# First layer norm's row factors sent through DRAM, its centring folded into the user weight, and another item order at the start

## The chip, the cores and the metric

The kernel runs on one core of one Trainium2 chip. A core has five engines with an instruction stream of their own: TensorE (PE in the profile, with its weight loads as PEld), VectorE (DVE), ScalarE (ACT), GpSimd (POOL) and SyncE (SP), and 16 DMA engines that the streams of SP and ACT feed. The metric is the device time of one execution in microseconds (us), less is better. Matrix data goes from DRAM to SBUF, products are summed up in PSUM banks of 512 floats a partition.

## The reference

```python
def layernorm(x): m = mean(x); v = var(x); return (x - m) / sqrt(v + 1e-5)      # over 128 features

h = item_feat @ W_item.T + b_item                     # items, 10000 x 128
b = layernorm(x) @ W_user.T + b_user                  # users, 10000 x 128
x = x + relu(adj @ h + b)                             # adj 10000 x 10000, float32, 400 MB
x = x + ffn(layernorm(x))                             # an LSTM over 10000 steps, gates on its output,
                                                      # cumulative sums from both sides
```

Reading `adj` once is 400 MB, and `adj @ h` is most of the arithmetic. The LSTM comes behind it and isn't touched by the change.

## The kernel before

**Layout.** Everything is held transposed: features on the 128 partitions, users along the free axis. `adj @ h` is computed in 20 blocks of 500 users (`NB`, `BW`), each in PSUM bank `psG[:, j % 2]`. A block sums over 78 chunks of 128 items and a tail of 16 items. The chunks come in 20 pieces of 4 or 3 (`r` = 0 to 19), and a piece in two halves (`h`) of 2 chunks: 500 KB of `raw`, one DMA. There are room for 4 pieces of `raw` and for 4 halves of `a_hi` and `a_lo`.

**Three matmuls a chunk.** Float32 values are split in a high part (type fp32r, made by ACT with a copy, `split_hi`) and a low part (DVE subtracts, `split_lo`). TensorE then multiplies high by high, low by high and high by low (the three lines 826 to 828). So each half passes DMA, ACT, DVE, PE in this order, and semaphores (`raw_in`, `hi_ready`, `lo_ready`, `halves_done`) tie them together. Each engine's order of work is written out by hand: the loop over `r` in `body` of each engine, with side work put in behind piece `AT[...]` (every block) or `FIRST[...]` (block 0).

**Items.** During block 0 the items are projected as well. A quad is 4 chunks (512 items, 256 KB; 20 quads). SP loads them in parts (`PARTS`) into `u`; TensorE projects quad `q` into `psI[:, q % 2]` (`item_quad`), DVE adds the bias (`item_sum_part`), ACT makes the high part (`item_hi_part`), DVE the low part (`item_lo_part`). Piece `r` of block 0 needs quad `r`; `item_quad(r + 3)` stands at the head of piece `r` on TensorE, and quads 0 to 2 stand ahead of block 0.

**First layer norm** (of x, one block ahead of its use). TensorE transposes the block's 500 users in 4 pieces of 125 into rows (`to_rows`, `psT`); DVE takes `bn_stats` of the rows, and forms the variance in three steps (`stats`, `pair_up`, `eps`); POOL raises it to the power -1/2 (`inv_std`, a 125x4 tile `rstd`); DVE forms the shift (`row_scale`); ACT scales and shifts the rows (`normalise`, 4 instructions); TensorE transposes back (`to_columns`, 4 transposes into `psV`); ACT copies to `v` (`out_v`); and TensorE adds `wu` times `v` to the block's sum at piece `AT["bias"]` = 2.

**Second layer norm** (of x + relu(...), one block behind) goes the same way through `psT`, `psV`, and ACT's `out_u`. A block of x1 is stored to DRAM by SP at `AT["store"]`, and the next block of x loaded at `AT["load"]`.

**Small loads** stand in ACT's queue: the weights, `late_loads(r)` among ACT's pieces of block 0.

## Time and profile before

| | |
|---|---|
| median of 3 runs | 1453.94 us (1453.23 to 1456.08) |
| profiled execution, its own time | 1454.52 us |
| its span, first to last instruction | 1452.7 us |
| granted TensorE clock, mean | 0.992 |
| busy: PE, DVE, ACT, POOL | 98%, 84%, 75%, 15% of the span |
| DMA, mean over the span | 295 GB/s |
| stage with the adjacency | about 0 to 1144 us |
| LSTM and output | from there to the end |

The page cuts the span into 40 slices of 36.3 us. In the first 31 of them TensorE is at nine tenths or more save the first, and the DMA engines move 323 to 396 GB/s; from then on DMA is nearly idle. The adjacency stage is 79% of the span.

### The profile page before, as it was taken

How to read it: one execution, taken by the hardware profiler on the slowest of the kernel's cores; microseconds unless marked ns; L12 is line 12 of the kernel's file. 1: busy time of each engine (PE TensorE's matmuls, PEld its weight loads, DVE VectorE, ACT ScalarE, POOL GpSimd, SP SyncE). 2: the span in 40 equal slices, each digit the busy share in tenths (PEclk: the TensorE clock that was granted, in tenths of full speed). 3: DMA queues.
4: the chain of work that ended last, by engine and by line, in shares of the span. 5: the costliest groups of instructions: out<-in, count | busy, mean ns of one | idle time of the engine just before them, and what ended most of it. 6: DMA issues, size and time to landing. Idle time of an engine off the chain costs nothing.

```text
span 1452.7 us, 26480 instructions
## 1 busy us (share of the span) xinstructions
PE 1420.6 (98%) x7556; PEld 1222.4 (84%) x7556; DVE 1221.7 (84%) x2051; ACT 1092.8 (75%) x1602; POOL 214.7 (15%) x193
## 2 busy tenths in 40 slices
PE   7999999999999999999999999999999899999994
PEld 6878888888888888888888888888888799999994
DVE  7998888888889888888888888888989666676667
ACT  5678778878878878887887887887788576556662
POOL 0000010001001001001000000100100132027775
PEclk9999999999999999999999999999999999999997
DMA  9899999999999999999999999999999203000003
GB/s 373 330 323 357 395 363 356 390 366 351 392 361 359 387 366 363 376 372 371 370 363 384 364 361 393 358 359 393 359 356 389 100 0 141 0 2 0 1 0 142
DMA packets 129397, 428.00 MB, mean 295 GB/s; under 512 B 15763, under 2 KB 30420, under 8 KB 129238
## 3 DMA queue, kind: packets, MB, share of 16 engines
q1 hardware_dynamic: 127776, 426.43, 77.8%
q10 hardware_dynamic: 1590, 1.18, 0.2%
q8 instruction: 17, 0.28, 0.1%
q14 instruction: 14, 0.11, 0.0%
HBM read 417.30 MB, written 10.24 MB: 294 GB/s over the span
## 4 chain that ended last, share of the span: by engine, by line
PE 91%; DVE 4%; POOL 2%; issue 2%; DMA 1%; ACT 0%; POOLq 0%; SPq 0%; DVEq 0%
PE psG L826 24%; PE psG L827 24%; PE psG L828 24%; PE psZ L948 8%; PE psZ L934 2%; PE psZ L936 2%; PE psZ L938 2%; DVE a_lo L1107 1%; PE psG L844 1%; PE psT L792 1%; PE psV L800 1%; PE psI L872 1%; POOL own L516 1%; PE psZ L954 1%; POOL own L519 1%
## 5 line engine op out<-in xcount | busy, mean ns | idle before, releaser
L619 ACT ACTIVATE a_hi<-raw 128x1000 fp32r<-128x1000 f32 (+1 forms) x800 | 812.6, 1031 | 221.7 <-PE psG L828 215.3
L1107 DVE TENSOR_TENSOR a_lo<-raw,a_hi 128x1000 fp32r<-128x1000 f32 (+1 forms) x800 | 907.1, 1169 | 68.4 <-ACT a_hi L619 56.0
L826 PE MATMUL psG<-a_hi,item_hi 128*128 128x500 f32 x1560 | 620.1, 398 | 1.0 <-DVE a_lo L1107 0.8
L827 PE MATMUL psG<-a_lo,item_hi 128*128 128x500 f32 x1560 | 605.4, 388 | 0.0
L828 PE MATMUL psG<-a_hi,item_lo 128*128 128x500 f32 x1560 | 604.0, 387 | 0.0
L826 PEld LDWEIGHTS psG<-a_hi,item_hi 128*128 128x128 f32 x1560 | 293.1, 188 | 62.5 <-issue 5.4
L827 PEld LDWEIGHTS psG<-a_lo,item_hi 128*128 128x128 f32 x1560 | 293.4, 188 | 58.7 <-issue 4.4
L828 PEld LDWEIGHTS psG<-a_hi,item_lo 128*128 128x128 f32 x1560 | 292.8, 188 | 59.1
L445 POOL TENSOR_TENSOR rstd<-var,minus_half 125x4 f32<-125x4 f32 x40 | 76.1, 1903 | 1048.9 <-DVE var L1089 1048.9
L948 PE MATMUL psZ<-hist,wh 128*128 (+1 forms) x1264 | 168.0, 276 | 1.2 <-DVE hist L1275 1.1
L948 PEld LDWEIGHTS psZ<-hist,wh 128*128 128x128 f32 x1264 | 155.1, 192 | 1.8 <-issue 1.6
L704 ACT ACTIVATE psZ<-psZ 128x250 f32<-128x250 f32 x158 | 57.4, 363 | 62.2 <-PE psZ L948 60.0
L936 PE MATMUL psZ<-u_lo,wx_hi 128*128 (+1 forms) x312 | 97.4, 314 | 0.0
L934 PE MATMUL psZ<-u_hi,wx_hi 128*128 (+1 forms) x312 | 93.7, 302 | 0.0
L938 PE MATMUL psZ<-u_hi,wx_lo 128*128 (+1 forms) x312 | 87.3, 281 | 0.0
L1076 DVE BATCH_NORM_STATS2 moments<-psT 125x6 f32<-125x128 f32 x156 | 34.7, 285 | 48.5 <-PE psT L792 48.5
L1275 DVE SCALAR_TENSOR_TENSOR hist<-go,psZ 128x125 f32 (+1 forms) x160 | 45.4, 284 | 35.6 <-ACT psZ L713 34.7
L1260 DVE SCALAR_TENSOR_TENSOR psZ<-psZ,C 128x125 f32<-128x125 f32 x158 | 46.5, 295 | 33.4 <-ACT psZ L704 31.3
L708 ACT ACTIVATE go<-psZ 128x250 f32<-128x250 f32 x158 | 59.4, 376 | 7.0 <-PE psZ L948 0.4
L713 ACT ACTIVATE psZ<-C 128x125 f32<-128x125 f32 x158 | 43.6, 276 | 24.6 <-DVE C L1270 21.0
L936 PEld LDWEIGHTS psZ<-u_lo,wx_hi 128*128 128x128 f32 x312 | 59.1, 190 | 0.8
L938 PEld LDWEIGHTS psZ<-u_hi,wx_lo 128*128 128x128 f32 x312 | 58.8, 189 | 0.8
(171 smaller groups left out, 840.6 us busy)
## 6 DMA issues: line engine op xcount, KB each, us to landing
raw<-in_adj_main SPq DMA_DIRECT2D x760, 500.0 KB, 5.7
raw<-in_adj_main SPq DMA_DIRECT2D x40, 250.0 KB, 3.3
x_copy<-xb SPq DMA_DIRECT2D x20, 250.0 KB, 5.8
u<-x_copy SPq DMA_DIRECT2D x1, 5000.0 KB, 14.5
out<-u SPq DMA_DIRECT2D x25, 200.0 KB, 2.4
xb<-in_xT SPq DMA_DIRECT2D x18, 250.0 KB, 5.3
u<-in_itemT SPq DMA_DIRECT2D x8, 512.0 KB, 10.7
raw<-in_adj_tail SPq DMA_DIRECT2D x60, 31.2 KB, 2.9
```

The lines of the kernel that those rows point to most:

```text
L445: pool.tensor_tensor(rstd[:, :], var[:, :], minus_half[0:SW, :].to_broadcast([SW, SUB]), ALU.pow).then_inc(ln_rstd, 1)
L619: nc.scalar.activation(a_hi[:, s % CUT, 0:n], raw[:, r % RAW, at:at + n], ACT.Copy)\
L704: nc.scalar.activation(tb(g, 0, 2).rearrange("p (q k) -> p q k", k=KG), zb(g, 0, par), ACT.Tanh)\
L708: nc.scalar.activation(go[:, g, :].rearrange("p (q k) -> p q k", k=KG), zb(g, 1, par), ACT.Tanh)\
L826: pe.matmul(bank, w_hi, hi, start=(c == 0), stop=False)
L827: pe.matmul(bank, w_hi, lo, start=False, stop=False)
L828: last = pe.matmul(bank, w_lo, hi, start=False, stop=False)
L934: pe.matmul(z, w_hi, hi, start=(q % 2 == 0), stop=False, skip_group_check=True)
L936: pe.matmul(z, w_hi, lo, start=False, stop=False, skip_group_check=True)
L938: pe.matmul(z, w_lo, hi, start=False, stop=False, skip_group_check=True)
L948: last = pe.matmul(psZ[:, 2 * par + bank, at:at + KG], wh[:, q * HID:(q + 1) * HID], hist[:, row, g * KG:(g + 1) * KG], start=False, stop= ...
L1107: last = dve.tensor_tensor(a_lo[:, s % CUT, 0:m], raw[:, r % RAW, at:at + m], a_hi[:, s % CUT, 0:m].bitcast(f32), ALU.subtract)
```

## The change

It has three parts.

1. **The first layer norm leaves its transposes back.** The mean is taken out by the weight: TensorE multiplies `centre` (identity minus 1/128) with `wu` once, at piece 3 of block 0, and DVE copies the product over `wu`. What is left is one factor 1/sqrt(v + eps) for each user, and users lie along the free axis. POOL writes it into a tile of its own, `rstd1` (125x4). ACT's queue stores that tile to DRAM (`send_rstd`, 125 packets of 16 bytes) and, four pieces later (three in block 0), loads it back to all 128 partitions (`spread_rstd`, 128 packets of 2000 bytes) into `factors`, which is the tile `sq`. DVE multiplies x by it into `v` (`scale_user`), reading the factors with a step of 4 floats. DVE's `row_scale`, ACT's four `normalise` instructions, TensorE's `to_columns` and ACT's `out_v` of this norm are gone.
2. **Places.** `scaled` is at piece 3, `bias` goes from piece 2 to 5, `rows1` to `eps1` one piece earlier, `load` from 11 to 10, `wx` from 10 to 12. In block 0 the bias goes from 7 to 11.
3. **The items at the start.** Parts of two quads from the first on, and they are loaded at every second piece from piece 3 on, where they were loaded behind each of the first nine pieces. Only quads 0 and 1 are projected ahead of block 0; quad 2 stands between the halves of piece 0 and quad 3 behind them. On ACT the first `split_hi` stands ahead of the first item part, and on DVE the first `split_lo` ahead of the low part of quad 0 and the sum of quad 1.

```diff
-PARTS = (0, 1, 3, 5, 7, 9, 11, 13, 15, 17, QUADS)
+PARTS = (0, 2, 4, 6, 8, 10, 12, 14, 16, 18, QUADS)
+PART_AFTER = {0: (1,), 1: (2,), **{2 * i - 3: (i,) for i in range(3, len(PARTS) - 1)}}
-AT = dict(relu=1, x1=2, bias=2, rows2=3, stats2=4, pair2=5, eps2=5, scale2=6, norm2=7, back2=8, out2=10,
-          rows1=12, stats1=13, pair1=14, eps1=14, scale1=15, norm1=16, back1=17, out1=19,
-          store=7, load=11, wx=10)
+AT = dict(relu=1, x1=2, scaled=3, bias=5, rows2=3, stats2=4, pair2=5, eps2=5, scale2=6, norm2=7, back2=8, out2=10,
+          rows1=11, stats1=12, pair1=13, eps1=13, send=15, spread=19, store=7, load=10, wx=12)
-FIRST = dict(rows=0, stats=1, scale=2, norm=3, back=4, out=5, bias=7)
+FIRST = dict(rows=0, stats=1, send=3, centre=3, centred=4, spread=6, scaled=9, bias=11)
...
+            def send_rstd(m):
+                act.wait_ge(ln_rstd, m + 1)
+                act.dma_start(rstd_dram[0:1, :].rearrange("o (p s) -> p (o s)", s=SUB), rstd1[:, :]).then_inc(rstd_stored, 16)
+            def spread_rstd(j):
+                act.wait_ge(rstd_stored, 16 * (j + 1))
+                act.dma_start(factors[:, :], rstd_dram[0:1, :].to_broadcast([P, BW])).then_inc(rstd_spread, 16)
...
+            def scale_user(j):
+                dve.wait_ge(rstd_spread, 16 * (j + 1))
+                by_row = factors[:, :].rearrange("p (r s) -> p s r", s=SUB)
+                xs, vs = (t.rearrange("p (s r) -> p s r", s=SUB) for t in (xb[:, j % 2, :], v[:, :]))
+                dve.tensor_tensor(vs, xs, by_row, ALU.mult).then_inc(v_ready, 1)
...
-                        if r + AHEAD < QUADS:
+                        if 0 < r < QUADS - AHEAD:
                             item_quad(r + AHEAD)
...
+                        if items and r == 0:
+                            item_quad(2 + h)
-                    if items and r == FIRST["back"]:
-                        to_columns(0)
+                    if items and r == FIRST["centre"]:
+                        pe.wait_ge(wu_in, 32)
+                        pe.matmul(psW[:, 0:HID], centre[:, :], wu[:, :], start=True, stop=True).then_inc(wu_psum, 1)
-                    if has1 and r == AT["back1"]:
-                        to_columns(2 * j + 1, u_ready if has2 else v_ready, j if has2 else 1)
...
+                    if items and r == FIRST["centred"]:
+                        dve.wait_ge(wu_psum, 1)
+                        dve.tensor_copy(wu[:, :], psW[:, 0:HID]).then_inc(wu_ready, 1)
```

How the order changes. VectorE's stream at the start of block 0, before (psI holds a projected quad, L1121 is its sum, L1107 the low part of a half of the adjacency, L1140 the low part of a quad):

```order
1 L1216 COPY bi<-psW 128x128
2 L1121 TENSOR_TENSOR u<-psI,bi 128x512 x2
3 L1140 TENSOR_TENSOR item_lo<-u,item_hi 128x512
4 L1107 TENSOR_TENSOR a_lo<-raw,a_hi 128x1000
5 L1121 TENSOR_TENSOR u<-psI,bi 128x512
6 L1107 TENSOR_TENSOR a_lo<-raw,a_hi 128x1000
7 L1140 TENSOR_TENSOR item_lo<-u,item_hi 128x512
8 L1107 TENSOR_TENSOR a_lo<-raw,a_hi 128x1000
```

and in the changed kernel (the same three are L1144, L1130, L1163):

```order
1 L1247 COPY bi<-psW 128x128
2 L1144 TENSOR_TENSOR u<-psI,bi 128x512
3 L1130 TENSOR_TENSOR a_lo<-raw,a_hi 128x1000
4 L1163 TENSOR_TENSOR item_lo<-u,item_hi 128x512
5 L1144 TENSOR_TENSOR u<-psI,bi 128x512
6 L1130 TENSOR_TENSOR a_lo<-raw,a_hi 128x1000
7 L1144 TENSOR_TENSOR u<-psI,bi 128x512
8 L1163 TENSOR_TENSOR item_lo<-u,item_hi 128x512
```

The first low part of the adjacency now stands behind one sum, where it stood behind two sums and the low part of quad 0.

TensorE's stream in the steady loop, before, at the end of piece 17 of a block (L826 to L828 are the three matmuls of a chunk, L800 the four transposes back of the first norm):

```order
520 L826 MATMUL psG<-a_hi,item_hi 128x500
521 L827 MATMUL psG<-a_lo,item_hi 128x500
522 L828 MATMUL psG<-a_hi,item_lo 128x500
523 L796 REGISTER_ALU
524 L800 MATMUL psV<-ident,normed 128x125 x4
525 L815 REGISTER_ALU
526 L826 MATMUL psG<-a_hi,item_hi 128x500
```

and at the same place in the changed kernel (L842 to L844):

```order
520 L842 MATMUL psG<-a_hi,item_hi 128x500
521 L843 MATMUL psG<-a_lo,item_hi 128x500
522 L844 MATMUL psG<-a_hi,item_lo 128x500
523 L831 REGISTER_ALU
524 L842 MATMUL psG<-a_hi,item_hi 128x500
```

The transposes and their wait are gone, and the next piece follows at once. The transposes back of the second norm, at piece 8, are still there.

VectorE's stream in the steady loop from the x1 sum (L1099) to the statistics of the second norm, before:

```order
115 L1099 TENSOR_TENSOR xb<-xb,un_bb 128x500
116 L1104 REGISTER_ALU
117 L1107 TENSOR_TENSOR a_lo<-raw,a_hi 128x1000
118 L1104 REGISTER_ALU
119 L1107 TENSOR_TENSOR a_lo<-raw,a_hi 128x1000
120 L1104 REGISTER_ALU
121 L1107 TENSOR_TENSOR a_lo<-raw,a_hi 128x1000
122 L1104 REGISTER_ALU
123 L1107 TENSOR_TENSOR a_lo<-raw,a_hi 128x1000
124 L1074 ISA
125 L1076 BN_STATS moments<-psT 125x6 x4
```

and in the changed kernel (L1122 is the x1 sum, L1130 the low part):

```order
116 L1122 TENSOR_TENSOR xb<-xb,un_bb 128x500
117 L1127 REGISTER_ALU
118 L1130 TENSOR_TENSOR a_lo<-raw,a_hi 128x1000
119 L1127 REGISTER_ALU
120 L1130 TENSOR_TENSOR a_lo<-raw,a_hi 128x1000
121 L1115 ISA
122 L1118 ISA
123 L1118 TENSOR_TENSOR v<-xb,sq 128x500
124 L1127 REGISTER_ALU
125 L1130 TENSOR_TENSOR a_lo<-raw,a_hi 128x1000
126 L1127 REGISTER_ALU
127 L1130 TENSOR_TENSOR a_lo<-raw,a_hi 128x1000
```

The multiplication at 123 is new, with its wait for the spread factors ahead of it; two halves' low parts and then the statistics are queued behind it.

## Rows read from the trace of the kernel before

**Rows 1.** The page: busy us, share and instructions of each engine.

```profile
PE 1420.6 (98%) x7556; PEld 1222.4 (84%) x7556; DVE 1221.7 (84%) x2051; ACT 1092.8 (75%) x1602; POOL 214.7 (15%) x193
```

**Rows 2.** Waits over the whole span: total us, times, longest.

```profile
ACT a_hi L619 <- PE psG L828: 215.3, 559, 2.8
...
ACT a_hi L619 <- DMA raw<-in_adj_main: 3.0, 5, 1.3
```

**Rows 3.** Windows: us, busy PE, PEld, DVE, ACT, POOL, clock, DMA, GB/s.

```profile
20.00:40.00 20.00, 19.82 (x109) 16.85 (x108) 19.90 (x33) 14.49 (x20) 2.04 (x2) 1.00 1.03 407
...
300.00:400.00 100.00, 100.00 (x456) 82.91 (x455) 88.48 (x111) 81.17 (x96) 5.79 (x3) 1.00 0.98 373
```

**Rows 4.** Timeline of TensorE in a steady block: start us, duration us.

```profile
570.53 0.60 PE L792 MATMUL psT<-ident,xb 128*125 128x128 f32 x4
...
604.74 0.39 PE L826 MATMUL psG<-a_hi,item_hi 128*128 128x500 f32 x1
...
614.66 0.39 PE L828 MATMUL psG<-a_hi,item_lo 128*128 128x500 f32 x1
614.89 0.59 PE L800 MATMUL psV<-ident,normed 125*128 125x125 f32 x4
...
615.55 0.39 PE L827 MATMUL psG<-a_lo,item_hi 128*128 128x500 f32 x1
...
626.14 0.60 PE L792 MATMUL psT<-ident,xb 128*125 128x128 f32 x4
```

**Rows 5.** Groups by line: busy us, mean ns, idle before.

```profile
L605 ACT ACTIVATE u<-psV 128x480 f32 (+1 forms) x19 | 20.1, 1060 | 0.0
...
L1099 DVE TENSOR_TENSOR xb<-xb,un_bb 128x500 f32 (+1 forms) x19 | 12.8, 672 | 0.0
...
L597 ACT ACTIVATE v<-psV 128x500 f32<-128x500 f32 x20 | 11.4, 571 | 2.4 <-PE psV L800 2.4
```

**Rows 6.** Timeline of TensorE from the start on, the lines that mark progress.

```profile
4.66 2.08 PE L872 MATMUL psI<-wi,u 128*128 128x128 f32 x8
9.62 3.52 PE L872 MATMUL psI<-wi,u 128*128 128x128 f32 x16 [2.89 <-DMA u<-in_itemT]
13.81 1.16 PE L872 MATMUL psI<-wi,u 128*128 128x128 f32 x8 [0.66 <-DMA u<-in_itemT]
14.72 0.47 PE L826 MATMUL psG<-a_hi,item_hi 128*128 128x500 f32 x1
...
26.65 0.48 PE L826 MATMUL psG<-a_hi,item_hi 128*128 128x500 f32 x1
```

**Rows 7.** Timeline of ScalarE, then of VectorE, in the same stretch.

```profile
8.11 1.95 ACT L619 ACTIVATE a_hi<-raw 128x1000 fp32r<-128x1000 f32 x2
...
11.74 0.69 DVE L1121 TENSOR_TENSOR u<-psI,bi 128x512 f32<-128x512 f32 x1 [4.20 <-PE psI L872]
...
12.95 1.19 DVE L1107 TENSOR_TENSOR a_lo<-raw,a_hi 128x1000 fp32r<-128x1000 f32 x1
```

**Rows 8.** DMA of the first 40 us: GB/s in slices of 1 us; issues with us to landing.

```profile
GB/s 0 33 247 349 358 402 405 409 392 260 319 410 412 428 416 414 416 415 412 410 400 409 402 406 401 411 413 413 421 413 413 394 404 412 400 413 413 391 391 418
...
raw<-in_adj_main SPq DMA_DIRECT2D x23, 500.0 KB, 10.2
u<-in_itemT SPq DMA_DIRECT2D x8, 512.0 KB, 10.7
```

**Rows 9.** DMA issues of the whole span: KB each, median us to landing.

```profile
x_copy<-xb SPq DMA_DIRECT2D x20, 250.0 KB, 5.8
```

**Rows 10.** DMA from 40 to 45 us, where 128 packets of 4 bytes run.

```profile
q10 hardware_dynamic: 144, 0.00, 1.7%
...
fwc<-in_fw ACTq DMA_DIRECT2D x1, 0.5 KB, 5.6
```

**Rows 11.** Timeline of VectorE in a steady block, around the second norm's statistics.

```profile
598.64 1.20 DVE L1107 TENSOR_TENSOR a_lo<-raw,a_hi 128x1000 fp32r<-128x1000 f32 x1
601.56 0.89 DVE L1076 BATCH_NORM_STATS2 moments<-psT 125x6 f32<-125x128 f32 x4 [1.71 <-PE psT L792]
```

More of the change, by code:

```diff
@@ L95, in program @@
     ds = bass.ds
+    rstd_dram = nc.dram_tensor("rstd_copy", (1, BW), f32).ap()
     x1_dram = nc.dram_tensor("x1_copy", (P, N), f32).ap()
@@ L163, in program @@
         rstd = sb("rstd", [SW, SUB], f32, first)
+        rstd1 = sb("rstd1", [SW, SUB], f32, first)
+        factors = sq
         shift_rows = sb("shift_rows", [SW, SUB], f32, first)
@@ L401, in load_block @@
                         sp.dma_start(xb[:, (j + 1) % 2, :], xT[:, ds((j + 1) * BW, BW)]).then_inc(xb_in, 16)
-            load_block(0, wait=False, move=False, items={r: (r + 1,) for r in range(len(PARTS) - 2)})
+            load_block(0, wait=False, move=False, items=PART_AFTER)
             with nc.sync.Fori(1, NB - 1) as j:
@@ L586, in relu, with normalise @@
                     .then_inc(relu_done, 1)
-            def normalise(m):
-                act.wait_ge(ln_scale, m + 1)
+            def normalise(count):
+                act.wait_ge(ln_scale, count)
                 for s in range(SUB):
@@ L631, in body @@
                         late_loads(r)
[L632 to L635 removed]
+                    if items and r == FIRST["send"]:
+                        send_rstd(0)
+                    if items and r == FIRST["spread"]:
+                        spread_rstd(0)
                     if has2 and r == AT["norm2"]:
[L637 removed]
+                        normalise(j)
                     if has2 and r == AT["out2"]:
[L639 to L643 removed]
+                        out_u(j, odd, pair)
+                    if has1 and r == AT["send"]:
+                        send_rstd(2 * j + 1)
+                    if has1 and r == AT["spread"]:
+                        if items:
+                            act.wait_ge(item_ready, QUADS)
+                        spread_rstd(j + 1)
             def item_hi_part(q):
@@ L787, in _, with to_rows @@
         def _(pe):
-            def to_rows(m, par):
-                if not (isinstance(m, int) and m == 0):
-                    pe.wait_ge(ln_normed, m)
+            def to_rows(par, reader=None, count=0):
+                if reader is not None:
+                    pe.wait_ge(reader, count)
                 for s in range(SUB):
@@ L1193, in body @@
                         eps(0)
-                    if items and r == FIRST["scale"]:
-                        row_scale(0)
+                    if items and r == FIRST["centred"]:
+                        dve.wait_ge(wu_psum, 1)
+                        dve.tensor_copy(wu[:, :], psW[:, 0:HID]).then_inc(wu_ready, 1)
+                    if items and r == FIRST["scaled"]:
+                        scale_user(0)
+                    if has2 and r == AT["scaled"]:
+                        scale_user(j)
                     if has2 and r == AT["x1"]:
@@ L1211, in body @@
                         eps(2 * j + 1)
-                    if has1 and r == AT["scale1"]:
-                        row_scale(2 * j + 1)
             dve.wait_ge(bi_psum, 1)
```

72 lines of the change are left out of this document (34 added, 38 removed).

## The prediction

> **What bounds the kernel now.** I read the page's busy shares first. TensorE is busy in 98% of the span, VectorE in 84%, ScalarE in 75% [rows 1]. A busy share alone doesn't prove a bound, so the list of waits comes next: ScalarE waited 215.3 us for TensorE to give back a slot of `a_hi`, and 3.0 us in all for the adjacency's DMAs [rows 2]. So the chain DMA, ACT, DVE, PE is held up from its end: TensorE is the bound, and the others wait for its slots. The windows say by how much. From 300 to 400 us PE is busy in all 100 us, DVE in 88.5, ACT in 81.2, and DMA moves 373 GB/s; from 20 to 40 us, with the items on top, DMA moves 407 GB/s and DVE is busy in 19.9 of 20 us [rows 3]. So there are two regimes: the steady blocks, bound by PE with 12% left on DVE and about 8% on DMA, and block 0's beginning, where DVE and DMA are full as well.
>
> The timeline of TensorE gives its pace: 44 starts from 604.74 to 614.66, 0.2255 us a matmul [rows 4]. From one block's transposes to rows at piece 12 (570.53) to the next's (626.14) are 55.61 us [rows 4]. In them lie 234 matmuls and the tail's one (52.99 us), two sets of transposes to rows, two sets back, and the bias. What leaves TensorE's stream there shortens the block.
>
> **The transposes back: 20 sets.** One set of 4 stands between the starts at 614.66 and 615.55 [rows 4]. Without it those two starts would be 2 x 0.2255 = 0.45 us apart, and they are 0.89 apart: a set costs 0.44 us. (The set's own 0.59 us [rows 4] is the other end, but its last part overlaps the next matmul.) There are 20 sets of the first norm, one a block: 20 x 0.44 = 8.8 us. The transposes to rows stay and cost the same one piece earlier. The bias matmul costs the same at piece 5 as at piece 2; it is what is left of the block, 55.61 - 52.99 - 4 x 0.44 = 0.86 us. The new block is 55.17.
>
> **What leaves ScalarE** is 4 `normalise` instructions and `out_v` (0.57 us, [rows 5]) a block, and what comes is two issues of DMAs in its queue. ACT waits for TensorE anyway, so I count nothing. Its new waits: at piece 15 for POOL's power, whose input DVE finishes at piece 13; at piece 19 for the store to land, 4 pieces after its issue. Behind them stand the next `split_hi`, and behind those DVE and PE; they hurt only if a landing takes more than the distance.
>
> **The round trip through DRAM.** Four pieces are 48 matmuls, 10.8 us, from store to load; from the load's issue to DVE's use at piece 3 of the next block there are four again. A DMA of 250 KB to DRAM took 5.8 us [rows 9]; a load of 128 packets of 4 bytes 5.6 us [rows 10]. Both hops fit with 5 us left. In block 0 the hops are 3 pieces of 12 matmuls and a quad, about 3.6 us each, again 10.8 us, but there the queues are full: loads of the adjacency took 10.2 us there and those of the items 10.7 [rows 8]. Those wait behind their own queue's backlog; ACT's small loads don't, as the 5.6 us at 41 us show. I take 6 to 7 us for each hop, so nothing is late.
>
> What the two transfers cost the DMA engines: the spread is 0.256 MB, 0.6 us at 407 GB/s [rows 3]. For packets of 16 bytes the nearest row is that of 144 packets (128 of 4 bytes and the completions) that took 1.7% of 16 engines in 5 us, 1.36 engine-us, 9 ns each [rows 10]: 125 are 1.2 engine-us. That was reading from DRAM, this writes to it, which no row shows at that size. With 20.6 MB a block (40 halves, the stored and the loaded block), DMA needs 50.6 us at 407 GB/s and has 55.2. So the additions may reach 4.6 us a block before DMA becomes the bound. I take them as hidden.
>
> The Trainium skill, page "DMA: Bandwidth & Descriptors" (sections "Specifications" and "Why a DMA increments its semaphore by 16 and not by 1"), says that below 512 bytes a write turns into a read and a write, and that a DMA runs on the largest number of engines up to 16 that divides its slowest dimension: for 125 partitions 5 engines with 25 packets each. By the 9 ns of rows 10 that would be 0.2 us on each of five engines, and the sum stays; no row here shows either. It makes the first rival below easier to come true, which I left at 0.03.
>
> **What comes to VectorE.** `scale_user` multiplies 128x500. The like instruction with plain steps is 0.672 us [rows 5]. Its factors are read with a step of 16 bytes. For steps of that kind no read on DVE is in the rows; on ACT, writing with a large step took 1.060 us for 480 elements against 0.571 for 500 plain ones [rows 5], 1.9 times. So the price is between 0.67 and 1.28 us; I take 0.7, nearest to the row of the same engine. It replaces `row_scale`. At piece 3 DVE has room: before the statistics at 601.56 it stood idle for 1.71 us, waiting for TensorE's transposes [rows 11]. Those come up to 0.86 us sooner now, since the bias stands behind them; 1.71 - 0.86 = 0.85 us of room is left, and `v` isn't needed before piece 5. Even 1.28 us overdraws it by 0.4, less than the 0.65 us that 12% of idle time are worth in two pieces. Hidden; zero in the steady blocks.
>
> The Trainium skill, page "SBUF — State Buffer" (the note on SBUF cachelines), says that SBUF has lines of 16 bytes and that each access that goes to a new line pays a penalty. Here every factor would be on a new line. By that rule the upper price holds, and by the plain row the lower; the sum is the same by both, block 0 apart, which is a rival below.
>
> **TensorE in block 0 gets one matmul more,** `centre` by `wu`, a 128x128 of the items' kind: a quad of 4 such took 0.91 us of stream (13.81 to 14.72 [rows 6]), so 0.25 us. DVE's copy of the result, 0.3 us, falls at piece 4.
>
> **The start.** Before, PE waits for quads 1 and 2 to land and projects them from 9.62 (after 2.89 us idle), DVE can add their bias at 11.74 after 4.20 us idle, and the first low part of the adjacency starts at 12.95, although ACT had made the first two high parts from 8.11 on [rows 6, 7]. The first adjacency matmul is at 14.72, the first of piece 3 at 26.65 [rows 6]. I run the new order through with the durations of these rows, in us:
> - Quads 0 and 1 come with one 512 KB DMA. From the rates in rows 8 the summed bytes are 0.63 MB at 4, 1.4 at 6, 2.2 at 8, 3.6 MB at 12, then 0.41 a us, and loads landed 1.5 us behind their place. So: items 5.4, first halves 7.1 and 8.7, quads 2 and 3 10.2, piece 1 12.0 and 13.3, quads 4 and 5 14.8.
> - PE projects quads 0 and 1 from 5.4 to 9.3, at the slow early pace of rows 6 (2.08 us for one). DVE: sum of 0 to 8.1, low part of half 0 (1.1) 8.3 to 9.4, low part of quad 0 to 10.0, sum of quad 1 to 10.6, half 1 to 11.8.
> - PE: half 0 from 10.1, quad 2, half 1 from 12.3, quad 3, rows, then quad 4 (landed 14.8), piece 1 from about 15.7. DVE goes on without a gap: quads, four `bn_stats`, the variance; half 4 is ready at 19.9, half 6 at 23.3. PE starts piece 3 at 23.8.
>
> So piece 3 starts 26.65 - 23.8 = 2.85 us earlier. From there on PE isn't starved: half 6 of the adjacency would land at 18.9, halves 8 and 10 at 23.4 and 25.8, each 2 to 3 us before DVE gets to it, since the items now take 0.26 MB a piece and not 0.5. Bounds: if the matmuls of the first half run at half pace, 1.4 us less; if DVE were the only limit from 8.3 on (12.95 - 8.3), up to 4.6. I take 2.85.
>
> **The sum:** 8.8 + 2.85 - 0.25 = 11.4 us. Profiled time 1454.52 - 11.4 = 1443.1; the median of the runs is 0.6 below the profiled one, so 1442.5. I add 0.3 for DVE's copy and multiplication in block 0, where DVE is full: **1442.8 us**. The LSTM behind it is the same, and I expect the same time of it.
>
> **Rivals.**
> 1. *DMA becomes the bound* (slower). For: the DMA share is 0.98 already; a load from one spot of DRAM by 128 packets and small writes are in no row. Against: 407 GB/s in block 0. It decides from 4.6 us of additions a block, with 0.6 for the spread, 4.0 are left for 125 packets of 16 bytes, 8 on each of 16 engines: 0.5 us a packet. At 1 us each a block needs 50.6 + 0.6 + 8 = 59.2, 3.6 more than the 55.61 of before; 19 x 3.6 = 68, less 2.6 at the start: 1519. By the skill's rule of five engines, above, it would decide from 4.0 / 25 = 160 ns a packet, an estimate.
> 2. *The round trip is late* (slower). It decides from landings of 10.8 us. The 10.2 to 10.7 us of rows 8 are close. If the spread takes 12 us in each block, DVE stalls 1.2 us, and its lead takes perhaps 0.4: (0.8 - 0.44) x 19 = +6.8, less 2.3 at the start: 1458. Late in block 0 alone: 1444.
> 3. *VectorE pays for the step, and block 0 gives less.* 0.6 us more for the multiplication at piece 9 of block 0, 1.4 for matmuls at half pace at the start, 0.5 that DVE doesn't catch up: 1445.3.
> 4. *The start gives nothing*, since DMA, full from 5 us on [rows 8], holds back block 0 whatever the order. Against it: ACT waited 3.0 us for loads [rows 2], with twice the items ahead of the adjacency. 1442.8 + 2.6 = 1445.4.
> 5. *The steady blocks give nothing*, since DVE's and DMA's loops, at 88% and 92% [rows 3], take over at once: 1453.9 - 2.6 = 1451.3.
>
> **How the numbers follow.** Forecast 0.60, rival 1 0.03, rival 2 0.06 (half of it slower, half in block 0 only), rival 3 0.13, rival 4 0.12, rival 5 0.06. Under 0.2% (2.9 us) I call it no change, about what can be told. Faster: 0.60 + 0.13 + 0.12 + half of rival 2, 0.03 = 0.88; same: 0.06; slower: 0.03 + 0.03 = 0.06. The forecast's own range is 1440.8 (the start's upper bound) to 1444.2; with rivals 3 and 4 to 1446, and part of 5: 1440.5 to 1448.
>
> **What would show it.** In the changed profile: 19 groups of transposes into `psV`, not 39; matmuls still 0.2255 us apart; the first adjacency matmul near 10 us and piece 3 near 24; the steady block shorter by 0.44 us; `v<-xb` at 0.7 (or 1.3) us, and little waiting for it on the spread; landings of the two new DMAs under 8 us. I am wrong if ACT waits for `raw` by tens of us in the steady blocks (rival 1), if DVE waits ahead of `v` (rival 2), or if PE waits for `a_lo` at every block's piece 3 or 4 (rivals 3, 5).

## The result, and the profile after

The changed kernel takes 1445.34 us (median of 4 runs, 1444.94 to 1446.79) against 1453.79 us (4 runs), a ratio of 0.994 with a 95% interval of 0.9928 to 0.9952. The forecast was 1442.8 us, its range 1440.5 to 1448.0. So it is faster, as forecast, by 8.45 us where 11.4 less 0.3 were expected. The profiled execution took 1444.94 us, its span is 1443.1.

The page's busy shares of the changed kernel answer to [rows 1]. TensorE has 78 instructions less: 80 transposes are gone, and the product of `centre` and `wu` shows as 2. VectorE has 21 us more:

```profile
PE 1412.8 (98%) x7478; PEld 1214.0 (84%) x7478; DVE 1242.8 (86%) x2052; ACT 1067.8 (74%) x1502; POOL 214.5 (15%) x193
```

The waits of the changed kernel (engine, what waited, for whom: us in all, times, longest) answer to [rows 2]. ScalarE still waits mostly for TensorE, but its waits for the adjacency's DMAs went from 3.0 us to 33.9, in 89 places:

```profile
ACT a_hi L634 <- PE psG L844: 208.4, 585, 2.8
...
ACT a_hi L634 <- DMA raw<-in_adj_main: 33.9, 89, 1.9
...
PEld psG L842 <- DVE a_lo L1130: 4.4, 11, 0.6
```

TensorE's timeline at the start (start, duration, engine, line, operation, tiles, count) answers to [rows 6]. The first matmul of the adjacency is at 10.03 where 10.1 was forecast, that of piece 3 at 24.09 where 23.8 was (26.65 before), and the centring takes 0.22 us (26.89 to 27.11):

```profile
5.39 3.78 PE L890 MATMUL psI<-wi,u 128*128 128x128 f32 x16
10.03 0.50 PE L842 MATMUL psG<-a_hi,item_hi 128*128 128x500 f32 x1 [0.86 <-DVE item_lo L1163]
...
15.90 0.48 PE L842 MATMUL psG<-a_hi,item_hi 128*128 128x500 f32 x1
...
24.09 0.47 PE L842 MATMUL psG<-a_hi,item_hi 128*128 128x500 f32 x1
...
26.89 0.38 PE L853 MATMUL psW<-wu,centre 128*128 128x128 f32 x2
27.11 1.06 PE L890 MATMUL psI<-wi,u 128*128 128x128 f32 x8
```

The multiplication by the factors, as the groups of instructions give it (busy us in all, mean ns of one, idle time before it): 1.075 us and no wait for the spread. The like instruction with plain steps takes 0.672 [rows 5]. The 19 groups of transposes into `psV` are there as 76:

```profile
L1118 DVE TENSOR_TENSOR v<-xb,sq 128x500 f32<-128x500 f32 x20 | 21.5, 1075 | 0.0
...
L816 PE MATMUL psV<-ident,normed 125*128 125x125 f32 x76 | 11.2, 270 | 0.0
```

The best ruler is the tail's matmul, the last of each block. In the changed kernel blocks 0 to 3 end here:

```profile
84.34 0.38 PE L835 MATMUL psG<-a_hi,item_hi 80*128 80x500 f32 x1
...
141.36 0.39 PE L835 MATMUL psG<-a_hi,item_hi 80*128 80x500 f32 x1
...
196.58 0.40 PE L835 MATMUL psG<-a_hi,item_hi 80*128 80x500 f32 x1
...
251.88 0.39 PE L835 MATMUL psG<-a_hi,item_hi 80*128 80x500 f32 x1
```

Beside the same line of before, in us:

| | before | after | gained | forecast |
|---|---|---|---|---|
| end of block 0 | 88.39 | 84.34 | 4.05 | 3.18 |
| block 1 | 55.79 | 57.02 | -1.23 | 0.44 |
| a steady block, undisturbed | 55.60 | 55.22 | 0.38 | 0.44 |
| blocks 2 to 18, sum | 945.26 | 939.51 | 5.75 | 7.48 |
| block 19 | 54.73 | 54.77 | -0.04 | 0 |
| end of the stage | 1144.17 | 1135.64 | 8.53 | 11.1 |

(3.18 is 2.85 + 2 x 0.44 - 0.25 - 0.3.) The LSTM behind it took 1.07 us less in this execution (307.46 us for 308.53). The change has no part in that: over the 14 profiled executions of this document what follows the stage takes either 307.3 to 307.5 us (six of them, the changed kernel's here among them) or 308.3 to 308.5 (eight, that of before among them). So of the 9.6 us between the two profiled executions 8.53 belong to the change.

So three things are to be explained: block 1 loses 1.8 us against a steady block; a set of transposes is worth 0.38 and not 0.44; and among the steady blocks there are stalls (one block takes 55.73 us), 0.77 us in all. In block 1 it is ScalarE that is late, for `raw`. Its timeline in the changed kernel, where before it had no wait for a DMA at all between 78 and 100 us:

```profile
85.77 0.66 ACT L595 ACTIVATE un_bb<-psG,bu 128x500 f32<-128x500 f32 x1
88.23 1.04 ACT L634 ACTIVATE a_hi<-raw 128x1000 fp32r<-128x1000 f32 x1 [1.80 <-DMA raw<-in_adj_main]
89.88 1.04 ACT L634 ACTIVATE a_hi<-raw 128x1000 fp32r<-128x1000 f32 x1 [0.61 <-DMA raw<-in_adj_main]
91.13 1.04 ACT L634 ACTIVATE a_hi<-raw 128x1000 fp32r<-128x1000 f32 x1 [0.21 <-DMA raw<-in_adj_main]
```

The spread was issued at 80.88 and landed 8.0 us later, in the midst of that. TensorE still had finished halves to work on; its first wait in block 1 comes 4 us after ScalarE fell idle at 86.4, for VectorE's low part:

```profile
90.56 0.50 PE L842 MATMUL psG<-a_hi,item_hi 128*128 128x500 f32 x1 [0.23 <-DVE a_lo L1130]
```

### The profile page after: what moved, and what is told of

Same layout as the page of the kernel before. It is cut to its first block, busy times and chain, and to the rows that moved or that the text cites. A ratio compares the mean times of both kernels' runs of the same rounds, so it can differ in the third digit from the quotient of the medians.

```text
span 1443.1 us, 26187 instructions
## 1 busy us (share of the span) xinstructions
PE 1412.8 (98%) x7478; PEld 1214.0 (84%) x7478; DVE 1242.8 (86%) x2052; ACT 1067.8 (74%) x1502; POOL 214.5 (15%) x193
## 4 chain that ended last, share of the span: by engine, by line
PE 91%; DVE 3%; issue 2%; POOL 2%; DMA 1%; ACT 0%; POOLq 0%; DVEq 0%; SPq 0%; ACTq 0%
PE psG L842 24%; PE psG L843 24%; PE psG L844 24%; PE psZ L965 8%; PE psZ L951 2%; PE psZ L953 2%; PE psZ L955 2%; PE psG L863 1%; PE psT L810 1%; PE psI L890 1%; DVE a_lo L1130 1%; POOL own L526 1%; PE psZ L971 1%; DMA raw<-in_adj_main 1%; POOL own L529 1%
## 5 line engine op out<-in xcount | busy, mean ns | idle before, releaser
L634 ACT ACTIVATE a_hi<-raw 128x1000 fp32r<-128x1000 f32 (+1 forms) x800 | 821.8, 1031 | 244.8 <-PE psG L844 208.4
L1130 DVE TENSOR_TENSOR a_lo<-raw,a_hi 128x1000 fp32r<-128x1000 f32 (+1 forms) x800 | 911.0, 1170 | 74.5 <-ACT a_hi L634 55.2
L842 PE MATMUL psG<-a_hi,item_hi 128*128 128x500 f32 x1560 | 620.5, 398 | 2.1 <-DVE a_lo L1130 1.1
L844 PE MATMUL psG<-a_hi,item_lo 128*128 128x500 f32 x1560 | 604.7, 388 | 0.0
L842 PEld LDWEIGHTS psG<-a_hi,item_hi 128*128 128x128 f32 x1560 | 293.5, 188 | 66.9 <-issue 5.6
L844 PEld LDWEIGHTS psG<-a_hi,item_lo 128*128 128x128 f32 x1560 | 293.2, 188 | 59.4
L951 PEld LDWEIGHTS psZ<-u_hi,wx_hi 128*128 128x128 f32 x312 | 59.0, 190 | 0.0
## 6 DMA issues: line engine op xcount, KB each, us to landing
u<-in_itemT SPq DMA_DIRECT2D x9, 512.0 KB, 10.1
```

Of the source, the lines that this page charges most:

```text
L634: nc.scalar.activation(a_hi[:, s % CUT, 0:n], raw[:, r % RAW, at:at + n], ACT.Copy)\
L842: pe.matmul(bank, w_hi, hi, start=(c == 0), stop=False)
L844: last = pe.matmul(bank, w_lo, hi, start=False, stop=False)
L951: pe.matmul(z, w_hi, hi, start=(q % 2 == 0), stop=False, skip_group_check=True)
L1130: last = dve.tensor_tensor(a_lo[:, s % CUT, 0:m], raw[:, r % RAW, at:at + m], a_hi[:, s % CUT, 0:m].bitcast(f32), ALU.subtract)
```

## The experiments

Theory A: TensorE's stream bounds the blocks, and what is lost is lost to the two new transfers, where VectorE and the ring of `raw` have no lead. Theory B: VectorE (1.08 us for the multiplication, and the new order) loses it. The times of before beside them are 1453.67 us (experiments 1 to 3), 1454.53 (4 to 7), 1454.78 (8 to 10) and 1454.45 (11 and 12). A table of all profiles stands behind the experiments.

**1. The new start alone**: the kernel before with part 3 of the change and nothing of parts 1 and 2.

```diff
-PARTS = (0, 1, 3, 5, 7, 9, 11, 13, 15, 17, QUADS)
+PARTS = (0, 2, 4, 6, 8, 10, 12, 14, 16, 18, QUADS)
+PART_AFTER = {0: (1,), 1: (2,), **{2 * i - 3: (i,) for i in range(3, len(PARTS) - 1)}}
...
-            item_quad(2)
...
```

> The kernel before with the new order of block 0 alone (parts of the items, two quads ahead of the adjacency, DVE's and ACT's order); the first norm keeps its transposes back. Theory A (PE, with a debt): the start gains 2.5 us at piece 3 and keeps nearly all of it; block 1 loses at most 0.5, because the loss of 1.7 us there comes with the spread. 1451.3 to 1451.8. Rival B (block 0 and 1 together have a bound of their own, DVE or DMA, which the earlier start only reaches sooner): block 1 gives back 1.5 us or more, and 1452.5 to 1453.3 is left.

Measured: 1451.9 us, ratio 0.999 (0.9981 to 0.9999). In its profile block 0 ends 2.52 us earlier, block 1 takes 55.78 us as before, and all is kept to the end of the stage (1141.65). Theory A's reading holds. The profiled execution is the fastest of the 11, though, and the median lies 0.1 us above the expected range: by the medians the start alone is worth 1.8 us.

```profile
85.87 0.39 PE L821 MATMUL psG<-a_hi,item_hi 80*128 80x500 f32 x1
...
141.65 0.39 PE L821 MATMUL psG<-a_hi,item_hi 80*128 80x500 f32 x1
```

**2. The factors alone**: the changed kernel with the start of before (the diff above the other way round).

> The changed kernel with the old order of block 0: only the row factors through DRAM. Theory A: steady blocks of 55.22 us, 0.39 less than before each, 18 x 0.39 = 7.0, block 0 shorter by 0.4 to 0.8, block 1 longer by 1 to 1.7 since the spread sits in its beginning: 1446.6 to 1447.4. Rival B: block 1 takes 55.2 to 55.5 and the kernel is 1445.8 to 1446.3, that is, start and factors together lose what each keeps alone.

Measured: 1448.87 us, ratio 0.9967 (0.9957 to 0.9978). Block 0 ends at 88.23, block 1 takes 55.38, the steady ones 55.22 with four stalls of 0.2 us and one of 0.5; the stage ends at 1138.48, 5.69 us earlier. That is neither expectation: block 1 hardly loses, as in B, but stalls of 1.4 us lie elsewhere, and ScalarE waits 32.3 us for `raw`. Neither part alone makes block 1 long. Block 0 gains only 0.16 us here; its first adjacency matmul starts at 15.74, 1.02 us later than before, and the first four start 0.41 to 0.57 us apart.

**3. The spread's bytes taken away.**

```diff
-                act.dma_start(factors[:, :], rstd_dram[0:1, :].to_broadcast([P, BW])).then_inc(rstd_spread, 16)
+                if isinstance(j, int) and j == 0:
+                    act.dma_start(factors[:, :], rstd_dram[0:1, :].to_broadcast([P, BW])).then_inc(rstd_spread, 16)
+                else:
+                    act.dma_start(factors[0:1, :], rstd_dram[0:1, :]).then_inc(rstd_spread, 16)
```

> The changed kernel, but from block 1 on the spread loads only one partition's row of factors (2 KB for 256 KB); the other partitions multiply by old values, so the first norm of blocks 1 to 19 is left wrong. Nothing else moves. If the spread's bytes delay the adjacency (theory A), block 1 falls from 57.0 to 55.5 us or less, ACT's 33.9 us of waits for raw fall below 15, and the time is 1443.0 to 1443.8. If they are hidden (rival: the prefetch ran dry by itself), block 1 stays within 0.3 of 57.0 and the time within 0.5 of 1445.3.

Measured: 1443.7 us, ratio 0.9933 (0.992 to 0.9947). Block 0 ends at 84.31 as in the changed kernel, block 1 takes 55.38, and every block from 2 to 18 takes 55.21 to 55.23. The stage ends 2.44 us earlier than in the changed kernel. ScalarE's waits in it:

```profile
ACT a_hi L637 <- PE psG L847: 226.8, 640, 2.8
...
ACT a_hi L637 <- DMA raw<-in_adj_main: 13.2, 24, 1.6
```

VectorE still pays its 1.08 us here, so theory B falls: with no spread beside the adjacency that price costs the steady blocks nothing and block 1 at most 0.16 us (before the change, too, block 1 was 0.19 us longer than a steady block). The windows from 84 to 88 us, and of their first half (busy time of each engine and count, granted clock, DMA share, GB/s), show what the spread does to its neighbours. First the changed kernel, then this one:

```profile
84.00:88.00 4.00, 4.00 (x19) 3.10 (x18) 3.91 (x4) 2.43 (x3) 0.00 (x0) 1.00 0.78 254
84.00:86.00 2.00, 2.00 (x10) 1.44 (x9) 2.00 (x3) 2.00 (x3) 0.00 (x0) 1.00 0.63 186
```

```profile
84.00:88.00 4.00, 4.00 (x19) 3.10 (x18) 4.00 (x5) 3.54 (x5) 0.00 (x0) 1.00 0.98 363
84.00:86.00 2.00, 2.00 (x10) 1.45 (x9) 2.00 (x3) 2.00 (x3) 0.00 (x0) 1.00 0.99 351
```

In these 4 us DMA moved 0.44 MB less with the spread in flight, although the 254 GB/s hold bytes of the spread too. In the first two of them the compute engines do the same work in both kernels, and 0.33 MB are missing already, so the gap isn't only the echo of a late ScalarE. The DMA share falls with the rate, 0.63 for 0.99: the DMA engines stood idle in part of that time. Why they did, no run shows. The forecast had counted the spread's bytes alone.

**4. 500 packets of 4 bytes and plain steps.**

```diff
-                act.dma_start(rstd_dram[0:1, :].rearrange("o (p s) -> p (o s)", s=SUB), rstd1[:, :]).then_inc(rstd_stored, 16)
+                with nc.allow_non_contiguous_dma(reason="500 packets of 4 bytes"):
+                    act.dma_start(rstd_dram[0:1, :].rearrange("o (s p) -> p (o s)", s=SUB), rstd1[:, :]).then_inc(rstd_stored, 16)
...
-                by_row = factors[:, :].rearrange("p (r s) -> p s r", s=SUB)
-                xs, vs = (t.rearrange("p (s r) -> p s r", s=SUB) for t in (xb[:, j % 2, :], v[:, :]))
-                dve.tensor_tensor(vs, xs, by_row, ALU.mult).then_inc(v_ready, 1)
+                dve.tensor_tensor(v[:, :], xb[:, j % 2, :], factors[:, :], ALU.mult).then_inc(v_ready, 1)
```

> The changed kernel with the factors stored transposed: 500 packets of 4 bytes in the place of 125 of 16, and scale_user reads them with plain steps. DVE's multiplication falls from 1.08 to 0.67 us. Theory (the spread's bytes are what block 1 pays, DVE has room): block 1 stays over 56.5 us, steady blocks 55.22, time within 0.5 of 1445.3; more small packets may make it longer, by 0.5 to 2 us over all. Rival (DVE's price of 1.08 us in block 1 is part of it): block 1 is 0.4 or more shorter, 1444.5.

Measured: 1550.31 us, ratio 1.0626 (1.0565 to 1.0687). Both expectations were wrong by 100 us. Blocks take 58.8 to 64.3 us, though VectorE's multiplication fell to 0.671. The store of 2 KB, issued at 622.34, nearly stops the adjacency; in these windows of that kernel the last two columns are the DMA share and GB/s:

```profile
624.00:626.00 2.00, 2.00 (x10) 1.66 (x9) 2.00 (x3) 1.36 (x3) 0.00 (x0) 1.00 1.36 292
626.00:628.00 2.00, 2.00 (x10) 1.69 (x9) 1.94 (x2) 1.69 (x2) 0.00 (x0) 1.00 1.03 43
628.00:630.00 2.00, 2.00 (x10) 1.67 (x9) 1.71 (x3) 1.42 (x2) 0.00 (x0) 1.00 1.23 36
630.00:632.00 2.00, 2.00 (x10) 1.65 (x10) 0.94 (x1) 0.00 (x0) 0.00 (x0) 1.00 0.50 32
632.00:634.00 2.00, 2.00 (x11) 1.46 (x9) 0.68 (x1) 0.62 (x1) 0.00 (x0) 1.00 0.51 103
634.00:636.00 2.00, 0.87 (x4) 0.41 (x3) 0.00 (x0) 0.00 (x0) 0.00 (x0) 1.00 0.91 281
```

Against 407 GB/s these windows lack 3.3 MB, 8 us of DMA for one store, by this estimate 16 ns of all 16 engines for each packet, where the forecast took 9 ns of one. (Against the steady 373 GB/s of [rows 3] it is 2.9 MB.) In block 0 ScalarE even waited 7.8 us for the store to land: with 500 packets the round trip is late once, as in the second rival. This is the first rival's mechanism; it is real, but the changed kernel's packets lie on its cheap side. In the changed kernel the store is issued at 624.31, and there is only a dip:

```profile
624.00:626.00 2.00, 2.00 (x11) 1.67 (x10) 2.00 (x3) 1.70 (x2) 0.28 (x1) 1.00 1.01 346
626.00:628.00 2.00, 2.00 (x11) 1.65 (x10) 2.00 (x3) 1.36 (x3) 0.00 (x0) 1.00 1.10 282
628.00:630.00 2.00, 2.00 (x10) 1.68 (x9) 1.93 (x2) 1.69 (x2) 0.00 (x0) 1.00 0.78 199
```

The profile's pages also count the packets of ScalarE's queue, for before, the changed kernel and this one in turn (packets, MB, share):

```profile
q10 hardware_dynamic: 1590, 1.18, 0.2%
...
q10 hardware_dynamic: 7070, 6.34, 1.6%
...
q10 hardware_dynamic: 14570, 6.34, 1.5%
```

A block has 274 packets more than before in the changed kernel, and 649 in this one. With 144 for the spread (128 and 16 completions, as the prediction reads [rows 10]), 125 + 5 and 500 + 5 are left for the store. Five completions for 16 speak for a store that runs on 5 of the 16 engines, as the prediction considered.

The Trainium skill, page "DMA: Bandwidth & Descriptors" (section "Specifications"), says that a write of less than 512 bytes is turned into a read and a write. The run agrees that small writes are dear; that it was this that stopped the other packets, no run here shows.

**5. One packet stored in the place of 125.**

```diff
+                if isinstance(m, int) and m == 0:
...
+                else:
+                    act.dma_start(rstd_dram[0:1, 0:SUB], rstd1[0:1, :]).then_inc(rstd_stored, 16)
```

> The changed kernel, but from block 0's piece 15 on the store writes only one partition's 4 factors (one packet of 16 bytes for 125); the first norm of blocks 1 to 19 is left wrong. Theory: the store is cheap, block 1 and the time stay within 0.5 us of 57.0 and 1445.3, and the spread still lands in 7 to 8 us. Rival (125 small writes cost the DMA engines as much as the spread): block 1 falls by 0.5 us or more, ACT's waits for raw from 33.9 us to under 20, 1444.2.

Measured: 1445.81 us, ratio 0.9939 (0.9922 to 0.9956). The time says the store is cheap, the profile says more: ScalarE's waits for `raw` fall to 10.0 us, and of blocks 2 to 18 all but one (55.62) take 55.21 to 55.24. Block 0 ended at 86.54, though, and block 1 took 55.40. The 2.2 us arise at the start, and they look like TensorE's clock. In this execution the adjacency's first matmuls start 0.42 us apart, 500 columns at 1.2 GHz, and in the changed kernel's profile 0.23 us, the level of 2.4 GHz. All of TensorE's work is slow there, the weight loads too (0.33 us for 0.19) and the quad behind the matmuls (1.91 us for 1.05), so it isn't a matter of operands that land late. But the granted clock reads 1.00 in both. TensorE had stood idle for 0.86 us ahead of them in both. The timeline of this kernel, and below it a weight load of the changed kernel:

```profile
10.02 0.79 PE L845 MATMUL psG<-a_hi,item_hi 128*128 128x500 f32 x1 [0.86 <-DVE item_lo L1166]
...
11.02 0.62 PE L847 MATMUL psG<-a_hi,item_lo 128*128 128x500 f32 x1
11.03 0.33 PEld L845 LDWEIGHTS psG<-a_hi,item_hi 128*128 128x128 f32 x1
11.44 0.62 PE L845 MATMUL psG<-a_hi,item_hi 128*128 128x500 f32 x1
11.86 0.62 PE L846 MATMUL psG<-a_lo,item_hi 128*128 128x500 f32 x1
```

```profile
10.60 0.19 PEld L842 LDWEIGHTS psG<-a_hi,item_hi 128*128 128x128 f32 x1
```

That costs block 0 2.2 us. Block 1 loses nothing here, so blocks 0 and 1 together end at 141.94, and at 141.36 in the changed kernel.

**6. The spread twice** (the second into `normed`, which is overwritten before it is read).

```diff
+                act.wait_ge(extra_in, 16 * count)
...
+                if not (isinstance(j, int) and j == 0):
+                    act.dma_start(normed[:, 0:BW], rstd_dram[0:1, :].to_broadcast([P, BW])).then_inc(extra_in, 16)
```

> The changed kernel with every spread from block 1's on issued twice (the second into a buffer that is overwritten before it is read): 256 KB more a block. If DMA is close behind PE (theory: the removed spread gave back 2.4 us), each steady block loses 0.3 to 1.5 us, block 1 1.5 us more, ACT's waits for raw rise over 100 us: 1452 to 1475. If the 4.6 us of room that the prediction counted are there, only block 1 pays (58.5) and the time is 1446.5 to 1447.5.

Measured: 1456.33 us, ratio 1.0006 (0.9996 to 1.0016). Steady blocks take 55.2 to 56.5 us, and ScalarE waits 55.3 us for `raw`; the wait for the second copy, which the edit adds ahead of `normalise`, shows in no row. One more quarter of a megabyte a block, 1.2% of its bytes, eats the whole gain. So the 4.6 us of room that the forecast counted aren't there for a spread.

**7. A set of transposes twice**, the second norm's.

```diff
-                for s in range(SUB):
+                for s in (*range(SUB), *range(SUB)):
                     last = pe.transpose(psV[:, s * SW:(s + 1) * SW], normed[0:SW, s * HID:(s + 1) * HID],
```

> The changed kernel with the second norm's 4 transposes back issued twice in blocks 1 to 19. It gives a set's price on TensorE by itself. By the starts in the trace of before (0.89 - 0.45) a set is 0.44 us, by the blocks' difference 0.39: a steady block of 55.66 or of 55.61 us, 19 times, and 1453.7 or 1452.7.

Measured: 1454.34 us, ratio 0.9999 (0.999 to 1.0009). The undisturbed blocks take 55.63 to 55.65 us, 0.42 more for a set. In the profile, whose execution is the slowest of the ten, stalls of 4.6 us come on top, up to 57.2 us a block. Perhaps a stretched block meets the transfers at other places; that is not shown.

**8. The changed kernel once more**, beside the next two.

> The changed kernel itself once more, for the spread between executions: block 0's last matmul was at 84.3 us in it and in one variant, and at 86.2 to 86.5 in two others whose block 0 is the same. Expected 1445.3 within 0.8; block 0 and 1 together end between 141.0 and 142.2 us whichever way block 0 falls, ACT's waits for raw are 25 to 40 us.

Measured: 1447.34 us (5 runs, 1446.98 to 1450.22), ratio 0.996 (0.9946 to 0.9973), 2 us above the first four. Blocks 0 and 1 end at 84.33 and 140.74, ScalarE waits 34.6 us for `raw`, and one steady block takes 57.16. The stage ends 1.41 us later than in the first profile: block 1 takes 0.61 less and the stalls 2.03 more. The other 1.0 us between the two profiled executions is the LSTM's longer time. So the changed kernel's time scatters by 2 us and more: through stalls that fall differently in each execution, and through the LSTM's two lengths.

**9. 16 packets of 128 bytes.** VectorE turns the 125x4 factors in a 128x32 tile into 4 rows of 32 for each of four groups of partitions; four DMAs store them, and the spread then has them in the order in which VectorE reads x. Two more things change with it: the multiplication has plain steps, and in the steady blocks the store stands one piece later (16 for 15).

```diff
+                by_quarter = rstd_dram[0, :].rearrange("(s b r) -> b s r", s=SUB, b=4)
+                for b in range(4):
+                    act.dma_start(by_quarter[b], turned[32 * b:32 * b + SUB, :]).then_inc(rstd_stored, 16)
...
+                dve.transpose(turned[:, :], rstd32[:, :]).then_inc(rstd_turned, 1)
...
-                by_row = factors[:, :].rearrange("p (r s) -> p s r", s=SUB)
+                by_row = factors[:, :].rearrange("p (s r) -> p s r", s=SUB)[:, :, 0:SW]
```

> The changed kernel with the factors turned by VectorE (one 32x32-block transpose of a 128x32 tile, before the store) and stored by 4 DMAs of 4 packets of 128 bytes in the place of one of 125 packets of 16 bytes; the spread has 2 KB rows as before, and scale_user reads with plain steps. Theory (each small packet written costs the DMA engines much more than its bytes; 4 bytes 500 times cost 8 us of them): ACT's waits for raw fall from 33.9 to 10 us, steady blocks all 55.22, multiplication 0.67 us, 1443.7 to 1444.6. Rival (VectorE's transpose and four issues on ScalarE's queue cost as much as they save; the store was never the trouble, the spread is): ACT's waits stay over 25 us, 1445 to 1446.5.

Measured: 1443.81 us (5 runs, 1443.42 to 1445.67), ratio 0.9933 (0.9919 to 0.9946), 3.5 us under the changed kernel in experiment 8, and its slowest run is under the other's fastest. Against the changed kernel's first measurement (1445.34, ratio 0.994) it is 1.5 us, or 1.0 by the ratios, and there the intervals overlap. Blocks 2 to 18 take 55.21 to 55.24 us without one stall, block 1 still 56.35. That the packets did it, and not the cheaper multiplication, rests on experiment 5, where the multiplication cost 1.07 us and the stalls were gone all the same. The groups of its two VectorE operations and its waits:

```profile
L1132 DVE TENSOR_TENSOR v<-xb,sq 128x500 f32<-128x500 f32 x20 | 13.5, 674 | 0.0
...
L1126 DVE STREAM_TRANSPOSE turned<-rstd 128x32 f32<-128x32 f32 x20 | 4.0, 202 | 0.0
```

```profile
ACT a_hi L642 <- PE psG L852: 226.3, 633, 2.8
...
ACT a_hi L642 <- DMA raw<-in_adj_main: 15.0, 33, 1.7
```

**10. The store twice** (the second to another place in DRAM).

```diff
+                act.dma_start(rstd_dram2[0:1, :].rearrange("o (p s) -> p (o s)", s=SUB), rstd1[:, :]).then_inc(rstd_stored, 16)
...
-                act.wait_ge(rstd_stored, 16 * (j + 1))
+                act.wait_ge(rstd_stored, 32 * (j + 1))
```

> The changed kernel with the store of the factors issued twice, the second time to another place in DRAM: 250 packets of 16 bytes a block for 125. If a small packet costs what packets4 showed (16 ns of the whole DMA each), a block has 2 us more of DMA, 54.8 of 55.2 us: ACT's waits for raw rise from 33.9 to over 80 us, steady blocks lose 0.2 to 1.5 us, 1449 to 1470. If only packets of 4 bytes are so dear, or the neighbours in one line of DRAM, nothing moves: 1445.3 within 1.

Measured: 1448.35 us (1444.89 to 1452.04), ratio 0.9951 (0.9936 to 0.9967), 1.0 over the changed kernel in experiment 8, less than the two kernels' runs scatter. ScalarE's waits stay at 30.9 us; the profiled execution, the slowest of the four, has stalls of 5 us in its steady blocks. The waits of over 80 us that follow from experiment 4's price of 16 ns of the whole DMA a packet didn't come, so that price doesn't carry over to packets of 16 bytes. What they cost is bounded, not settled: taking them away ends the stalls (experiments 5 and 9), doubling them adds a microsecond or nothing.

**11 and 12. TensorE kept busy at the start**, in the changed kernel and in that of experiment 9.

```diff
+            def keep_on(n):
+                for _ in range(n):
+                    pe.matmul(spare[:, 0:P], centre[:, :], ident[:, :], start=True, stop=True)
...
+            keep_on(10)
             pe.wait_ge(bi_in, 16)
...
             item_quad(1)
+            keep_on(8)
```

> The changed kernel with matmuls that nobody reads on TensorE: 10 of 128x128 ahead of the first bias row (TensorE idles there until 4.7 us) and 8 behind the second quad of items (it idles 0.86 us there). In three of the eight traces with the new start the adjacency's first 6 matmuls ran at half pace (0.42 us apart for 0.2255), and block 0 ended at 86.2 us for 84.3. Theory: it is TensorE's clock, which the fill keeps up: quads 0 and 1 take 2.1 us for 3.78, the first adjacency matmul is at 9.0 to 9.6, block 0 ends at 83.3 to 84.3 in every run, but block 1 gives part of it back, for DVE has no lead there: 1444.0 to 1445.3. Rival: the pace has another cause (operands still landing), the first matmuls stay as they are; 1445.5 to 1447.

> The kernel with 16 packets of 128 bytes (rows16) and the same fill on TensorE. If both parts add up, 1442.3 to 1443.4, with steady blocks of 55.22 us and ACT's waits for raw under 20 us. If the earlier start is all given back in block 1, 1443.8 as rows16.

Measured: 1448.21 us, ratio 0.9952 (0.9939 to 0.9965), and 1444.52 us, ratio 0.9932 (0.9919 to 0.9944): no gain in either. The pace did what the theory said, but I had the fill's length wrong: a float32 matmul counts twice in the profile, so 10 were 20 and took until 6.80 us, where 4.7 was to be reached. The timeline of experiment 11:

```profile
2.23 4.64 PE L879 MATMUL unused_bank<-ident,centre 128*128 128x128 f32 x20 [2.23 <-POOL centre L446]
6.80 0.53 PE L901 MATMUL psW<-bi_row,ones 1*128 1x128 f32 x2
7.25 2.05 PE L894 MATMUL psI<-wi,u 128*128 128x128 f32 x16
9.14 1.95 PE L879 MATMUL unused_bank<-ident,centre 128*128 128x128 f32 x16
10.98 0.50 PE L842 MATMUL psG<-a_hi,item_hi 128*128 128x500 f32 x1
11.32 0.39 PE L843 MATMUL psG<-a_lo,item_hi 128*128 128x500 f32 x1
```

The two quads take 2.05 us and not 3.78, and the adjacency starts at full pace, but 0.95 us late. Block 0 ends at 85.29 and 85.37, block 1 takes 55.39 in both. A fill half as long wasn't tried.

**The profiles side by side**, in us: end of block 0, length of block 1, what blocks 2 to 18 take above 55.22 each, pace of the adjacency's first matmuls, ScalarE's waits for `raw`. (In experiment 7 55.64 is taken for 55.22, in experiment 1 and before 55.60, the steady block there. In experiment 4 the tail's loads, 16.3 us, are counted with the waits.)

| | block 0 | block 1 | stalls | first matmuls | waits |
|---|---|---|---|---|---|
| before | 88.39 | 55.79 | 0.1 | full | 3.0 |
| 1, new start alone | 85.87 | 55.78 | 0.1 | full | 2.8 |
| 4, 500 packets | 90.46 | 60.71 | 102.6 | full | 125.5 |
| changed kernel | 84.34 | 57.02 | 0.8 | full | 33.9 |
| 8, again | 84.33 | 56.41 | 2.8 | full | 34.6 |
| 3, spread of one row | 84.31 | 55.38 | 0.0 | full | 13.2 |
| 9, packets of 128 bytes | 84.58 | 56.35 | 0.1 | full | 15.0 |
| 6, spread twice | 84.56 | 57.43 | 9.4 | full | 55.3 |
| 11, fill | 85.29 | 55.39 | 3.7 | full | 26.5 |
| 12, fill, 128 bytes | 85.37 | 55.39 | 0.0 | full | 8.9 |
| 5, one packet | 86.54 | 55.40 | 0.4 | half | 10.0 |
| 10, store twice | 86.13 | 56.91 | 5.1 | half | 30.9 |
| 7, set twice | 86.20 | 56.78 | 4.6 | half | 37.4 |
| 2, old start | 88.23 | 55.38 | 1.4 | half | 32.3 |

## Why the prediction was right, and where its terms were off

**TensorE as the bound: right.** Undisturbed steady blocks got shorter when work left TensorE's stream, and as long again when experiment 7 put a set in. **The size of a set was off:** 0.38 us by the blocks of before and after, 0.42 by experiment 7, for 0.44 by two starts [rows 4]. Over blocks 2 to 18 that is 7.48 - 5.75 - 0.77 (stalls) = 0.96 us of the missing 2.6. Why an added set costs more than a removed one is open; the other side work changed its place with the removal.

**The start: right.** Its 2.85 us came as 2.56 at piece 3, and 2.52 were kept when it was alone (experiment 1). The steps came as worked out: the second half's matmuls at 12.31 for 12.3, piece 1 at 15.90 for 15.7. The first quad at 5.39 for 5.4 holds some luck: TensorE waited for the bias row there, until 4.70, and not for the items. Block 0 as a whole gained 4.05 for 3.18. The 0.87 us more are open: the start alone gave 2.52 and the factors alone 0.16, with a late first matmul (experiment 2). Why both together give 4.05, no run shows. The bound of half pace, 1.4 us less, was not idle: it came true in experiments 5, 7 and 10, where block 0 ends 1.8 to 2.2 us later; of the changed kernel's own two profiles neither shows it.

**"I take them as hidden": this step failed.** The forecast weighed the two transfers by bytes and by the average of a block: 50.6 + 0.6 us of DMA for 55.2. (A block's 20.0 MB of adjacency with its two blocks of 0.256 MB are 20.5 MB, not 20.6; that changes nothing.) Three things were wrong with it.
- The spread costs its neighbours more than its bytes (experiment 3: 0.44 MB in 4 us), and a second one cost 9 to 11 us over the whole kernel (experiment 6, against 1447.34 and 1445.34), or 7 to 10 by the ratios.
- The average isn't what counts. VectorE is full until the end of block 0 (3.89 of 4 us from 80 to 84) and has little lead over TensorE, so loads of `raw` that come late in block 1 stop TensorE 4 us later (90.56). Block 1 came out 1.67 us worse than forecast. Without the spread (experiment 3) or without the new start (1 and 2) block 1 takes 55.4 to 55.8. That an end of block 0 a microsecond later is enough was only argued: experiments 5, 11 and 12 say so, 7 and 10 speak against it. Which execution pays there stays open.
- Small packets written hold up other traffic: 4 bytes 500 times do it plainly (experiment 4), 16 bytes 125 times only together with the spread. With both the steady blocks have stalls of 0.8 to 3.7 us in four profiles (the changed kernel, 8, 11, 2); with either taken away 0.0 to 0.4 in four (3, 5, 9, 12). Each is one execution, and the spread of times among a kernel's runs is as large.

The sum at the stage's end: 11.10 forecast, +0.87 in block 0, -1.67 in block 1, -0.96 for the sets, -0.77 for stalls, -0.04 in the last block: 8.53, as measured. The forecast's error of 2.5 us in the time holds these misses of both signs; that the +0.87 of block 0 made up for half of block 1's loss was luck.

**VectorE's price: inside the bounds, the value taken wrong, and it didn't matter.** 1.075 us, 1.6 times the plain 0.672, for 0.7 taken and bounds of 0.67 and 1.28. The Trainium skill, page "SBUF — State Buffer" (the note on SBUF cachelines), says each access to a new 16-byte line pays. The trace agrees in so far as this read, with a step of 16 bytes, is dearer: the plain-step variants (0.671, 0.674) put the price at 0.40 us. Other steps were not run. It was hidden, as argued (experiment 3).

**The rivals.** The round trip was never late: the spread landed after 6.1 to 8.0 us, for 6 to 7 taken, and nobody waited for it. The first rival's sign "ACT waits for `raw` by tens of us in the steady blocks" came true at 19 us between 200 and 1100, without DMA being the bound; as a test it was drawn too wide, since such waits are taken up by ScalarE's own slack (TensorE was busy in 899.98 of these 900 us).
